# Expert blocks taken by their number inside each expert, with the last stage's first group begun among the final blocks

## The chip, the cores and the metric

One core of a Trainium2 chip runs the whole program in one launch. The metric is the device time in microseconds (us); lower is better. The engines named below are TensorE (PE), VectorE (DVE), ScalarE (ACT), GpSimd (POOL) and SyncE (SP), which only issues DMAs.

## What is computed

`x` has 8192 tokens (128 graphs of 64) of 128 features. Four layers follow each other:

```
x = x + adj @ (LN(x) @ W0) + b0                       # graph layer 0
x = x + FFN0(LN(x))       # attention in each graph; then top 2 of 8 experts (hidden 341) for each token
x = x + norm(adj) @ (LN(x) @ W1) + b1                 # graph layer 1
x = x + FFN1(LN(x))       # top 2 of 6 experts, each three 128x128 layers
```

The part that matters here is the 8-expert layer. For every token, with weights of its two best experts,

```
for e in range(8):
    hh = silu(flat @ w1[e].T) * (flat @ w3[e].T)
    out = out + weights[:, e:e+1] * (hh @ w2[e].T)
```

is needed, and `out` is all that graph layer 1 waits for.

## The kernel before

Tokens are handled in 16 groups of 512 (four tiles of 128). The program has two large parts with a barrier of all five engines between them.

**Part A** (to about 400 us) computes graph layer 0, attention and the choice of experts for all groups. As it goes, POOL scatters each token's row (L358) into `slots_in` in DRAM, at a slot of the chosen expert: each expert has a region of `REG` = 65 rows of blocks, a block being 128 slots, filled in the order of the tokens. At the end the counts are final, and a chain of small DVE instructions (L903 to L924; `link` makes each wait for the one before) turns them into `table`: for each of the `NBLK` = 136 blocks its expert and its row in `slots_in`. The blocks stand expert after expert, the empty ones last. Beside that chain PE runs 18 filler matmuls (L1195) whose results nobody reads; POOL finishes its scatters; SP and ACT write zeros behind each expert's last row. Then comes the barrier (its instructions have the line L243).

**The middle stage** is a pipeline over the 136 blocks. `blocks` calls `block_of(k, u)` on every engine: SP loads block k into `xs` (L1342); PE transposes it (L1930); ACT and DVE split it into a high and a low part (L1488, L1590); PE multiplies by `w13` (L1938); ACT applies silu and DVE the product (L1478, L1595); PE transposes that (L1946) and multiplies by `w2` (L1923); DVE copies the result to `ys` (L1601); SP stores two blocks at a time to `slots_out` (L1345). Blocks 0 to 7 are written out, the rest is a loop of four blocks, and up to `skew` further calls drain the pipeline. During blocks 4 to 7 DVE also does `real_slots`: a token's slot in the region layout becomes its slot in the packed order of `slots_out`. POOL, in `weights()`, loads and splits the weights of the last stage, and then waits.

**The last stage** (`sweep`) runs graph layer 1 and the 6-expert layer, software-pipelined over the 16 groups. Step i of an engine does different work for groups i, i-1, i-2 and so on, in the order of its `body`. For a group g:

- DVE `pick` copies the slots; POOL `gt(0..7)` gathers the two expert rows of each token from `slots_out` (L1427, eight indirect DMAs). For group 0 it first waits until all blocks are stored.
- DVE `add0`, `add1` (L1646, L1655) form x2; `st0`, `mv0`, `var0` its statistics; POOL `rstd0` (L1445) the root; DVE `scale`, `xn_` (L1694).
- PE `aT` (L1968), ACT `tT_` (L1510), PE `gnn` (L1979), with POOL `xb_` (L1437) beside them; DVE `x3` (L1703), `st1`, `mv1`, `var1`; POOL `rstd1` (L1452); DVE `f3_` (L1735). From there on the 6-expert layer, which is nearly all PE's.

PE has filler matmuls `fill(11)`, `fill(10)` and `fill(2)` (L1955) around group 0's `aT`, `gnn` and the transposes of f3 (L1990).

Of the kernel before, what the change touches and what calls it, by code (L numbers as in the profile page):

```python
# [42 lines left out]
C_BLK, C_TRI8 = 592, 592 + NBLK  # L43
# [3 lines left out]
def constants():  # L47
# [14 lines left out]
    c[:, C_BASE:C_BASE + 8] = np.arange(8) * REG * P  # L62
    c[:, C_BLK:C_BLK + NBLK] = np.arange(NBLK)
# [30 lines left out]
def build(nc, x, adj_t, gnn0_w, gnn0_b, ln1, ln2, wqkv, wo, router0, w13, w2, gnn1_w, gnn1_b,  # L94
# [11 lines left out]
    def first(g):  # L106
        return isinstance(g, int) and g == 0

    with ExitStack() as whole:
# [20 lines left out]
        table = sb("table", [1, 2, NBLK], i32)  # L130
        slots_f, gaps = sb("slots_f", [P, NG, 2 * TG]), sb("gaps", [P, 8])


        with ExitStack() as ctx:
# [36 lines left out]
            cnti, nblk = sb("cnti", [P, 8], i32), sb("nblk", [P, 8])  # L171
            tri_nb, cum = sb("tri_nb", [1, 8, 8]), sb("cum", [1, 8])

            past, pastn = (sb(n, [1, NBLK, 8]) for n in ("past", "pastn"))
            bexp, bprev, brow = sb("bexp", [1, NBLK]), sb("bprev", [1, NBLK]), sb("brow", [1, NBLK])
# [67 lines left out]
            with nc.Block() as block:  # L243
# [281 lines left out]
                def _(dve):  # L525
# [370 lines left out]
                    def link(ins):  # L896
# [5 lines left out]
                    dve.wait_ge(router.sem, router.at("car", NG - 1))  # L902
                    link(V.tensor_copy(carry_b[:, :], carry[:, :]))  # L903
# [5 lines left out]
                    link(V.tensor_tensor(tri_nb[:, :, :], nblk[0:1, :].unsqueeze(1).broadcast_to([1, 8, 8]),  # L909
                                         cst[0:1, C_TRI8:C_TRI8 + 64].rearrange("p (a b) -> p a b", a=8), ALU.mult))  # L910
                    link(V.reduce_sum(cum[:, :], tri_nb[:, :, :], AX.X))
                    link(V.tensor_tensor(past[:, :, :], cst[0:1, C_BLK:C_BLK + NBLK].unsqueeze(2).broadcast_to([1, NBLK, 8]),
                                         cum[:, :].unsqueeze(1).broadcast_to([1, NBLK, 8]), ALU.is_ge))
                    link(V.tensor_tensor(pastn[:, :, :], past[:, :, :], nblk[0:1, :].unsqueeze(1).broadcast_to([1, NBLK, 8]), ALU.mult))
                    link(V.reduce_sum(bexp[:, :], past[:, :, :], AX.X))
                    link(V.reduce_sum(bprev[:, :], pastn[:, :, :], AX.X))
                    link(V.tensor_tensor(brow[:, :], cst[0:1, C_BLK:C_BLK + NBLK], bprev[:, :], ALU.subtract))

                    link(V.scalar_tensor_tensor(brow[:, :], bexp[:, :], float(REG), brow[:, :], ALU.mult, ALU.add))
                    link(V.tensor_scalar(table[:, 1, :], brow[:, :], float(P), None, ALU.mult))  # L920
                    link(V.tensor_scalar(table[:, 0, :], bexp[:, :], float(NE0 - 1), None, ALU.min))


                    link(V.tensor_scalar(gaps[:, :], nblk[:, :], -float(REG), float(P), ALU.add, ALU.mult))  # L924
                @block.tensor
                def _(pe):
# [267 lines left out]
                    for n in range(18):  # L1194
                        T.matmul(banks[1][:, 0:2 * P], ident, cst[:, 0:2 * P], start=True, stop=True)  # L1195


        with ExitStack() as ctx:
# [129 lines left out]
            with nc.Block() as block:  # L1328
                @block.sync
                def _(sp):  # L1330
# [16 lines left out]
                    blocks(sp, block_of, 8)  # L1347
# [29 lines left out]
                    def body(g, p):  # L1377
                        lda(g[0], p[0])
                        gst(g[1], p[1])
                        gld(g[1], p[1])  # L1380
                        store(g[2])
                    sweep(sp, body)
# [3 lines left out]
                def _(pool):  # L1386
# [784 lines left out]
```

## Time and profile before

| | us |
|---|---|
| median of 3 runs | 1071.14 |
| their range | 1069.75 to 1075.84 |
| the profiled execution, its own time | 1076.23 |
| its span, first to last instruction | 1074.4 |

PE is busy for 963.5 us (90%) of the span, DVE 721.2, ACT 574.8, POOL 461.3. The span divides into part A (to the barrier at 401), the middle stage (to 697), a passage in which group 0 gets through the start of the last stage (to 730), and the rest of the last stage (to 1074). "Busy" is a share of time in which an engine has an instruction in it; "PEclk" in the rows is the TensorE clock granted, as a share of 2.4 GHz, and is 1.0 or 0.5 at any moment.

### The profile page before, as it was taken

The page shows a single profiled execution, that of the slowest core. Times are in us where ns is not written, and L with a number is a line of the kernel's source. Part 1 is how long each engine was busy: PE and PEld are TensorE (multiplying, and loading weights), DVE is VectorE, ACT ScalarE, POOL GpSimd, SP SyncE. Part 2 cuts the span into 40 slices and gives each one's busy share as a digit, 9 for nine tenths or more (in the row PEclk, how much of TensorE's full clock was granted, in tenths as well). Part 3 has the DMA queues.
Part 4 walks back from the last instruction along what each step waited for, and adds up shares of the span by engine and source line. Part 5 has one row for each costly group of instructions (what it writes and reads, how often), then busy time and mean ns, then how long its engine had stood idle before and what let it go on. Part 6 is the DMA issues. An engine that isn't in the chain of part 4 may idle for free.

```text
span 1074.4 us, 26532 instructions
## 1 busy us (share of the span) xinstructions
PE 963.5 (90%) x6751; PEld 758.7 (71%) x6752; DVE 721.2 (67%) x3045; ACT 574.8 (54%) x1499; POOL 461.3 (43%) x459
## 2 busy tenths in 40 slices
PE   5888888888888759999999999938999999999998
PEld 4776777777776648999999999835555555555564
DVE  4677777677877655555555555427788888888864
ACT  2567667666676514555555555503455555555564
POOL 2256666656666568000000000076565665665510
PEclk9889898889999888999999999968999999999999
DMA  5211111111111014212212212122333433433332
GB/s 195 76 36 42 51 35 42 39 39 48 38 39 32 22 57 110 62 59 66 61 59 66 61 59 66 44 52 62 128 102 105 162 107 98 152 120 101 112 124 79
DMA packets 87453, 80.79 MB, mean 75 GB/s; under 512 B 26766, under 2 KB 80416, under 8 KB 85104
## 3 DMA queue, kind: packets, MB, share of 16 engines
q1 hardware_dynamic: 77472, 61.72, 18.1%
q0 software_dynamic: 8784, 18.16, 5.8%
q10 hardware_dynamic: 1152, 0.39, 0.2%
q8 instruction: 18, 0.29, 0.1%
q14 instruction: 27, 0.22, 0.1%
HBM read 57.50 MB, written 22.74 MB: 75 GB/s over the span
## 4 chain that ended last, share of the span: by engine, by line
PE 39%; issue 11%; POOL 9%; DVE 2%; ACT 1%; DMA 0%; POOLq 0%; DVEq 0%; SPq 0%; ACTq 0%
PE bank L1938 12%; PE bank L1923 9%; POOL expert_rows L1427 7%; PE bank L1946 4%; PE bank L2074 3%; PE bank L2066 3%; PE bank L2042 2%; PE bank L1930 1%; POOL rs_c L1445 1%; PE bank L1979 1%; PE bank L1968 1%; POOL xb_c L1437 1%; PE bank L2009 0%; ACT h L1496 0%; DVE base_all L1703 0%
## 5 line engine op out<-in xcount | busy, mean ns | idle before, releaser
L1427 POOL DMA_INDIRECT expert_rows<-slots_out,slot_c x128 | 140.6, 1099 | 34.9 <-issue 34.9
L1595 DVE TENSOR_TENSOR prod<-bank,act 128x342 f32<-128x342 f32 x136 | 70.0, 515 | 115.6 <-ACT act L1478 115.4
L358 POOL DMA_INDIRECT slots_in<-flat,slot_now x128 | 128.2, 1002 | 43.0 <-issue 43.0
L1426 POOL TENSOR_TENSOR spare_c<-mhalf 128x1 f32<-128x1 f32 x16 | 3.0, 185 | 274.0 <-DMA slots_out<-ys 274.0
L1923 PE MATMUL bank<-w_sb,prodT 128*128 x816 | 119.5, 283 | 0.6 <-DVE ys L1601 0.6
L1478 ACT ACTIVATE act<-bank 128x342 f32<-128x342 f32 x136 | 62.0, 456 | 96.0 <-PE bank L1938 96.0
L1923 PEld LDWEIGHTS bank<-w_sb,prodT 128*128 128x128 f32 x816 | 101.5, 191 | 7.5 <-issue 1.4
L1938 PE MATMUL bank<-w_hi,xT_hi 128*128 x272 | 99.5, 366 | 0.0
L2066 PE MATMUL bank<-h,ew 128*128 128x512 f32 x192 | 97.6, 605 | 0.0
L1938 PE MATMUL bank<-w_hi,xT_lo 128*128 x272 | 87.6, 322 | 0.0
L1938 PE MATMUL bank<-w_lo,xT_hi 128*128 x272 | 87.3, 321 | 0.0
L1503 ACT ACTIVATE h<-bank,eb 128x512 f32<-128x512 f32 x96 | 65.6, 685 | 29.2 <-DVE ys L1752 17.5
L2042 PE MATMUL bank<-f_hi,ew_hi 128*128 128x512 f32 x96 | 66.1, 688 | 6.9 <-ACT h L1496 5.8
L1496 ACT ACTIVATE h<-bank,eb 128x512 f32<-128x512 f32 x96 | 63.6, 680 | 13.8 <-PE bank L2042 13.5
L1946 PE MATMUL bank<-cst,prod 128*128 128x128 f32 x408 | 66.6, 272 | 0.1
L1483 ACT ACTIVATE prodT<-bank 128x384 f32<-128x384 f32 x136 | 66.0, 486 | 0.8 <-PE bank L1946 0.8
L450 ACT ACTIVATE pr<-sc,nmx 128x64 f32<-128x64 f32 x256 | 62.7, 335 | 1.9 <-DVE nmx L683 1.8
L1488 ACT ACTIVATE xT_hi<-bank 128x128 fp32r<-128x128 f32 x136 | 37.7, 278 | 44.5 <-PE bank L1930 44.5
L1590 DVE TENSOR_TENSOR xT_lo<-bank,xT_hi 128x128 fp32r<-128x128 f32 x136 | 39.7, 292 | 25.3 <-ACT xT_hi L1488 16.4
L1452 POOL TENSOR_TENSOR rs_d<-var_d,mhalf 128x4 f32<-128x4 f32 x16 | 18.0, 1124 | 86.4 <-DVE var_d L1727 86.4
L1946 PEld LDWEIGHTS bank<-cst,prod 128*128 128x128 f32 x408 | 52.9, 140 | 2.7 <-DVE prod L1595 0.3
L1938 PEld LDWEIGHTS bank<-w_lo,xT_hi 128*128 128x128 f32 x272 | 52.5, 193 | 0.0
(284 smaller groups left out, 2531.3 us busy)
## 6 DMA issues: line engine op xcount, KB each, us to landing
gate_bc<-gates_dram SPq DMA_DIRECT2D x16, 1536.0 KB
xs<-slots_in SPq DMA_DIRECT2D x136, 64.0 KB, 1.8
slots_out<-ys SPq DMA_DIRECT2D x68, 128.0 KB, 1.9
base_all<-in_x SPq DMA_DIRECT2D x16, 256.0 KB, 2.8
out<-ob SPq DMA_DIRECT2D x16, 256.0 KB
w_lo<-in_w SPq DMA_DIRECT2D x1, 2736.0 KB, 10.1
adjt<-in_adj_t SPq DMA_DIRECT2D x32, 64.0 KB, 2.3
slots_in<-flat,slot_now POOLq DMA_INDIRECT x128
```

The source lines that it names most:

```text
L358: G.indirect_dma_start(out=slots_in, out_offset=bass.IndirectOffsetOnAxis(ap=slot_now[p][:, n:n + 1], axis=0), in_=flat[p][:, n // 2, :], ...
L450: last = S.activation(pr[:, t, h, :], sc[:, t, h, :], ACT.Exp, scale=SCALE, bias=nmx[:, t * NH + h:t * NH + h + 1])
L1427: G.indirect_dma_start(out=rows[p][:, n, :], out_offset=None, in_=slots_out, in_offset=bass.IndirectOffsetOnAxis(ap=slot_now[p][:, n:n + 1 ...
L1483: S.activation(prodT[:, (u - 3) % 2, :], banks[5 + (u - 3) % 2][:, 0:KC * P], ACT.Copy).then_inc(prodT_copied, 1)
L1496: S.activation(h1[n % 3][:, :], banks[B_A[n]][:, :], ACT.Relu, bias=eb1[:, n:n + 1]).then_inc(per["ra"].sem, 1)
L1503: S.activation(h2[n % 3][:, :], banks[B_B[n]][:, :], ACT.Relu, bias=eb2[:, n:n + 1]).then_inc(per["rb"].sem, 1)
L1595: V.tensor_tensor(prod[:, u % 2, 0:HIDP], banks[3 + u % 2][:, 0:HIDP], act1[:, u % 2, :], ALU.mult).then_inc(prod_done, 1)
L1923: last = T.matmul(banks[7][:, 0:C], prodT[:, u % 2, n * P:(n + 1) * P], w2_sb[:, bass.ds(e * (KC * C) + n * C, C)], start=n == 0, stop=n = ...
L1938: last = T.matmul(banks[1 + 2 * n + par][:, 0:HIDP], xx[:, par, :], ww[:, bass.ds(e * (2 * HIDP) + n * HIDP, HIDP)], start=q == 0, stop=q ...
L1946: last = T.transpose(banks[5 + u % 2][:, n * P:(n + 1) * P], prod[:, u % 2, n * P:(n + 1) * P], ident)
L2042: last = T.matmul(banks[B_A[n]][:, :], ww[:, w], ff[p][:, :], start=q == 0, stop=q == 2)
L2066: T.matmul(banks[B_B[n]][:, :], ew2[:, n * C:(n + 1) * C], h1[n % 3][:, :], start=True, stop=True).then_inc(per["b"].sem, 1)
```

## The change

1. The order of the blocks. Before: all blocks of expert 0, then of expert 1, and so on. After: block 0 of every expert that has one, then block 1 of every expert, and so on, empty blocks last. Since the regions are filled in token order, the rows of group g now all lie in the first `filled(g)` = 32(g+1) blocks. The table is found by a longer chain (`dve_t` counts to 27 in place of 17), whose last two links wait for four small new matmuls. PE's fillers at that place become 12, the four matmuls, and 22.
2. `real_slots` has eight steps (blocks 4 to 11) in place of four, since slot numbers are mapped in another way; `pick` of groups 0 and 1 follows at blocks 12 and 13.
3. POOL's gathers for group g wait for `filled(g)` blocks only.
4. `blocks` writes out blocks 0 to 15 and 120 to 135. Between the last ones DVE does `add0` to `xn_` of group 0 and `add0` to `var0` of group 1 (`ahead`), SP loads both groups' `adj`, and after the last h matmuls PE does `aT` and `gnn` of group 0, in banks 0 and 1. `later(g, n)` takes this work out of the sweep.
5. `fill(11)` and `fill(10)` are gone; `fill(8)` stands ahead of the sweep.

```diff
+LEAD, LOOPED = 16, 120
@@ end of part A, DVE
-link(V.tensor_tensor(past[:, :, :], cst[0:1, C_BLK:C_BLK + NBLK].unsqueeze(2).broadcast_to([1, NBLK, 8]),
-                     cum[:, :].unsqueeze(1).broadcast_to([1, NBLK, 8]), ALU.is_ge))
...
+link(V.tensor_tensor(upto[:, :, :], nblk[:, :].unsqueeze(1).broadcast_to([P, MB, 8]),
+                     cst[:, C_JS:C_JS + MB].unsqueeze(2).broadcast_to([P, MB, 8]), ALU.min))
+link(V.reduce_sum(below[:, :], upto[:, :, :], AX.X))
+link(V.tensor_tensor(reached[:, :, :], pos.unsqueeze(2).broadcast_to([P, 2, MB]),
+                     below[:, :].unsqueeze(1).broadcast_to([P, 2, MB]), ALU.is_ge))
+link(V.reduce_sum(row_no[:, :], reached[:, :, :], AX.X))
...
+dve.wait_ge(pe_t, 2)
+link(V.tensor_scalar(table[:, 0, :], banks[2][0:1, 0:2 * P], float(NE0 - 1), None, ALU.add))
+link(V.tensor_scalar(table[:, 1, :], banks[2][0:1, 2 * P:4 * P], float(DUM), float(P), ALU.add, ALU.mult))
@@ middle and last stage
-for k in range(8):
+for k in range(LEAD):
     body(k, k % 4)
-with engine.Fori(2, NBLK // 4) as j:
+with engine.Fori(LEAD // 4, LOOPED // 4) as j:
...
-for k in range(NBLK, NBLK + skew):
+for k in range(LOOPED, NBLK + skew):
     body(k, k % 4)
+def filled(g):
+    return min(8 * TG * (g + 1), NBLK) if isinstance(g, int) else NBLK
+def later(g, n):
+    return None if isinstance(g, int) and g < n else g
@@ POOL, gt
-if first(g):
+if isinstance(g, int) and g < 5:
     for j in range(2):
-        pool.wait_ge(st[j], NBLK // 4 * 16)
+        pool.wait_ge(st[j], filled(g) // 4 * 16)
@@ SP
+if isinstance(k, int) and LOOPED < k <= LOOPED + 2:
+    lda(k - LOOPED - 1, k - LOOPED - 1)
@@ ACT
+if isinstance(k, int) and k == NBLK + 1:
+    tT_(0)
@@ DVE
+def ahead(k):
+    if 4 <= k < 12:
+        real_slots(k - 4)
+    elif k == 12:
+        dve.wait_ge(real, 11)
+        pick(0, 0)
+    elif k == 13:
+        pick(1, 1)
+    elif k == LOOPED:
+        dve.wait_ge(prepared, 8)
+        add0(0, 0)
+    elif k == LOOPED + 1:
+        add1(0, 0)
...
+    elif k == LOOPED + 6:
+        xn_(0)
+    elif k == LOOPED + 11:
+        add0(1, 1)
...
+    elif k == LOOPED + 14:
+        mv0(1)
+        var0(1)
+    elif k == NBLK + 3:
+        x3(0, 0)
+        st1(0)
+        mv1(0)
+        var1(0)
@@ PE
-    if first(g):
-        pe.wait_ge(at["add0"], 1)
-        fill(11)
...
+if isinstance(k, int) and k == NBLK:
+    pe.wait_ge(prepared, 8)
+    pe.wait_ge(lo_done, NBLK)
+    aT(0, 0)
+elif isinstance(k, int) and k == NBLK + 1:
+    pe.wait_ge(prod_done, NBLK - 1)
+    gnn(0)
...
+fill(8)
 sweep(pe, body)
```

PE's fillers at the end of part A. In the kernel before, PE's rows there are:

```order
L1193 MATMUL bank0<-carry_b,oneb 128x8 [waits dve_t]
L1195 MATMUL bank1<-cst 128x256 x18
L243 UNCONDITIONAL_BRANCH
L1909 UNCONDITIONAL_BRANCH [waits barrier_Pool_Activation_PE_DVE_SP_release]
L1930 MATMUL bank0<-cst,xs 128x128 [waits ld_slots0]
```

In the changed kernel:

```order
L1213 MATMUL bank0<-carry_b,oneb 128x8 [waits dve_t]
L1215 MATMUL bank1<-cst 128x256 x12
L1218 MATMUL bank2<-cst,entry 1x128 [waits dve_t]
L1218 MATMUL bank2<-cst,entry 1x128 x3
L1221 MATMUL bank1<-cst 128x256 x22
L247 UNCONDITIONAL_BRANCH
L2008 UNCONDITIONAL_BRANCH [waits barrier_Pool_Activation_PE_DVE_SP_release]
L2029 MATMUL bank0<-cst,xs 128x128 [waits ld_slots0]
```

Sixteen more fillers and the four matmuls on `entry` now stand ahead of PE's arrival at the barrier.

PE from the last blocks into the last stage (`w2_sb` rows are the second expert product, `cst,prod` the transposes, `cst` alone a filler). Before:

```order
L1946 MATMUL bank6<-cst,prod 128x128 x2
L1923 ISA [waits y_copied,prodT_copied]
...
L1923 MATMUL bank7<-w2_sb,prodT 128x128
L1955 MATMUL bank1<-cst 128x256 [waits add0,prepared]
L1955 MATMUL bank1<-cst 128x256 x10
L1968 MATMUL bank2<-adjt_c0,xn_c 128x128 [waits xn,ld_adj_c0]
L1968 MATMUL bank2<-adjt_c0,xn_c 128x128 x3
L1979 MATMUL bank6<-gw1,tT_c 128x128 [waits tT]
L1979 MATMUL bank6<-gw1,tT_c 128x128 x3
L1955 MATMUL bank1<-cst 128x256 x10
L1990 MATMUL bank5<-cst,f3 128x128 [waits f3]
```

After:

```order
L2063 MATMUL bank0<-adjt_c0,xn_c 128x128 [waits ld_adj_c0,xn,lo_done,prepared]
L2063 MATMUL bank0<-adjt_c0,xn_c 128x128 x3
L2022 ISA [waits y_copied,prodT_copied]
...
L2045 MATMUL bank6<-cst,prod 128x128 [waits prodT_copied,prod_done]
L2045 MATMUL bank6<-cst,prod 128x128 x2
L2074 MATMUL bank1<-gw1,tT_c 128x128 [waits tT,prod_done]
L2074 MATMUL bank1<-gw1,tT_c 128x128 x3
L2022 ISA [waits y_copied,prodT_copied]
...
L2053 MATMUL bank3<-cst 128x256 x8
L2083 MATMUL bank5<-cst,f3 128x128 [waits f3]
```

Both graph products of group 0 moved in among the last three `w2` products, and the next thing after the fillers is the transpose of f3.

DVE at the same place (`bank7` to `ys` is a block's result). Before:

```order
L1601 COPY ys<-bank7 128x128 [waits st_slots1,pe_y] x2
L1638 COPY slot_c0<-slots_all 128x8 [waits prepared,real_slots]
L1639 COPY gate_c0<-gates_all 128x8
L1638 COPY slot_c1<-slots_all 128x8
L1639 COPY gate_c1<-gates_all 128x8
L1646 SCALAR_TENSOR_TENSOR x2a<-expert_rows0,gate_c0,base_all 128x128 [waits gathered0]
```

After:

```order
L1644 COPY ys<-bank 128x128 [waits st_slots1,pe_y] x2
L1756 SCALAR_TENSOR_TENSOR base_all<-bank,deg,xb_c 128x128 [waits xb,gnn]
L1756 SCALAR_TENSOR_TENSOR base_all<-bank,deg,xb_c 128x128 x3
L1684 MEMSET spare_d 128x1 [waits x3]
L1764 BN_STATS st_d<-base_all 128x6 x4
```

Behind the last block's copy DVE goes straight to `x3` of group 0.

## Rows read from the trace of the kernel before

**Rows 1.** Stretches: length, busy us (instructions) of each engine, clock, DMA.

```profile
core 0: us, PE busy (x) PEld busy (x) DVE busy (x) ACT busy (x) POOL busy (x), PEclk, DMA share, GB/s
440.00:460.00 20.00, 20.00 (x153) 19.45 (x152) 10.48 (x30) 10.31 (x28) 0.00 (x0) 1.00 0.22 62
700.00:720.00 20.00, 5.35 (x13) 4.31 (x14) 5.29 (x22) 0.00 (x0) 15.31 (x17) 0.50 0.19 50
740.00:750.00 10.00, 9.28 (x36) 6.78 (x35) 7.58 (x48) 5.05 (x9) 4.23 (x6) 0.66 0.19 59
850.00:1000.00 150.00, 148.31 (x589) 87.21 (x588) 129.10 (x598) 82.34 (x145) 92.35 (x88) 1.00 0.38 121
```

**Rows 2.** The barrier's instructions (L243): durations in ns, and when they started.

```profile
L243 PEldq DRAIN  x1: 5490/5490/5490, 394.1 to 394.1; - x1
...
L243 POOLq DRAIN  x1: 1375/1375/1375, 399.6 to 399.6; - x1
...
L243 PEldq EVENT_SEMAPHORE  x1: 51/51/51, 401.1 to 401.1; - x1
```

**Rows 3.** Timeline, end of part A: start, duration, engine, line, shapes, count.

```profile
383.99 0.68 DVE L720 TENSOR_TENSOR base_all<-f,base_all 128x512 f32<-128x512 f32 x1
...
387.96 10.14 PE L1195 MATMUL bank<-cst 128*128 128x256 f32 x36
...
388.81 0.17 DVE L908 CAST nblk<-cnti 128x8 f32<-128x8 int32 x1
...
390.81 1.28 DVE L914 TENSOR_TENSOR pastn<-past,nblk 1x1088 f32<-1x1088 f32 x1
...
392.13 1.27 DVE L915 TENSOR_REDUCE bexp<-past 1x136 f32<-1x1088 f32 x1
```

**Rows 4.** Stretches of one microsecond around the barrier, columns as in rows 1.

```profile
392.00:393.00 1.00, 1.00 (x6) 0.88 (x5) 0.96 (x2) 0.00 (x0) 0.95 (x1) 0.86 0.63 196
...
402.00:403.00 1.00, 0.00 (x0) 0.00 (x0) 0.00 (x0) 0.48 (x1) 1.00 (x5) 0.76 0.03 8
409.00:410.00 1.00, 1.00 (x8) 0.94 (x8) 0.00 (x0) 0.44 (x2) 1.00 (x3) 0.83 0.93 85
```

**Rows 5.** PE's block transposes (L1930): ns min/median/max, first and last start.

```profile
L1930 PE MATMUL bank<-cst,xs x136: 272/273/477, 404.0 to 690.0; 128*128 128x128 f32 x136
```

**Rows 6.** Timeline, DVE between blocks: a step of `real_slots`.

```profile
412.34 1.08 DVE L1609 TENSOR_TENSOR gate_bc<-slots_f,cst 128x896 f32<-128x896 f32 x1
```

**Rows 7.** Timeline, the last block's `w2` product and its copy.

```profile
696.27 0.93 PE L1923 MATMUL bank<-w_sb,prodT 128*128 x6 [0.57 <-DVE ys L1601]
697.24 0.29 DVE L1601 COPY ys<-bank 128x128 f32<-128x128 f32 x1 [1.21 <-PE bank L1923]
```

**Rows 8.** Timeline from the last block to group 0's f3, and on.

```profile
701.38 1.20 POOL L1427 DMA_INDIRECT expert_rows<-slots_out,slot_c  x1 [0.65 <-issue]
...
713.36 1.14 DVE L1646 SCALAR_TENSOR_TENSOR x2a<-expert_rows,gate_c,base_all 128x128 f32<-128x128 f32 x4 [15.53 <-DMA expert_rows<-slots_out,slot_c]
...
718.75 2.89 DVE L1694 TENSOR_SCALAR xn_c<-x,mv_c,xscale 128x128 f32<-128x128 f32 x4
719.75 1.28 POOL L1437 TENSOR_TENSOR xb_c<-x,gb 128x512 f32<-128x512 f32 x1
...
722.09 1.05 PE L1968 MATMUL bank<-adjt_c,xn_c 128*128 128x128 f32 x8
...
723.89 1.16 PE L1979 MATMUL bank<-gw,tT_c 128*128 128x128 f32 x8 [0.75 <-issue]
...
725.09 1.13 DVE L1703 SCALAR_TENSOR_TENSOR base_all<-bank,deg,xb_c 128x128 f32<-128x128 f32 x4 [3.44 <-issue]
...
727.83 1.08 POOL L1452 TENSOR_TENSOR rs_d<-var_d,mhalf 128x4 f32<-128x4 f32 x1 [2.91 <-DVE var_d L1727]
...
732.30 1.01 POOL L1427 DMA_INDIRECT expert_rows<-slots_out,slot_c  x1 [0.30 <-issue]
...
734.65 1.05 POOL L1445 TENSOR_TENSOR rs_c<-var_c,mhalf 128x4 f32<-128x4 f32 x1
```

More of the change, by code:

```diff
@@ L1193, in _ @@
                     T.matmul(banks[0][:, 0:8], oneb[:, :], carry_b[:, :], start=True, stop=True).then_inc(pe_t, 1)
-                    for n in range(18):
+                    for n in range(12):
+                        T.matmul(banks[1][:, 0:2 * P], ident, cst[:, 0:2 * P], start=True, stop=True)
+                    pe.wait_ge(dve_t, 25)
+                    for n in range(4):
+                        last = T.matmul(banks[2][0:1, n * P:(n + 1) * P], entry[:, n // 2, n % 2:n % 2 + 1], ident, start=True, stop=True)
+                    last.then_inc(pe_t, 1)
+                    for n in range(22):
                         T.matmul(banks[1][:, 0:2 * P], ident, cst[:, 0:2 * P], start=True, stop=True)
@@ L1509, in tT_ @@
                                 act.wait_ge(at["gnn"], g)
-                            S.activation(tT[:, :, :], banks[B_AT][:, :], ACT.Copy).then_inc(at["tT"], 1)
+                            S.activation(tT[:, :, :], banks[0 if first(g) else B_AT][:, :], ACT.Copy).then_inc(at["tT"], 1)
                     def hi(g, p):
@@ L1616, in real_slots @@
-                            V.reduce_sum(back, gap, AX.X).then_inc(real, 1)
-                        else:
-                            dve.wait_ge(real, 3)
-                            V.tensor_tensor(slots_all[:, :, :].rearrange("p g s -> p (g s)"), slots, back, ALU.add).then_inc(real, 1)
-                    def block_and_slots(k, u):
-                        block_of(k, u)
-                        if isinstance(k, int) and 4 <= k < 8:
-                            real_slots(k - 4)
-                    blocks(dve, block_and_slots, 4)
@@ L1702, in x3 @@
                             for t in range(TG):
-                                last = V.scalar_tensor_tensor(stream(g, t), banks[B_GNN][:, t * P:(t + 1) * P], deg[p][:, t:t + 1], xb[:, t, :], ALU.mult, ALU.add)
+                                last = V.scalar_tensor_tensor(stream(g, t), banks[1 if first(g) else B_GNN][:, t * P:(t + 1) * P], deg[p][:, t:t + 1], xb[:, t, :], ALU.mult, ALU.add)
                             last.then_inc(at["x3"], 1)
@@ L1750, in m @@
                                 dve.wait_ge(gates_loaded[p], pair(g, p))
+                                if first(g):
+                                    for j in range(2):
+                                        dve.wait_ge(st[j], NBLK // 4 * 16)
                             reused(dve, "c", n, g)
@@ L1884, in body @@
                         dtop_(g[2])
-                        xn_(g[1])
+                        xn_(later(g[1], 1))
                         z_(g[2])
@@ L1967, in aT @@
                             for t in range(TG):
-                                last = T.matmul(banks[B_AT][:, t * P:(t + 1) * P], xn[:, t, :], adjt[p][:, t, :], start=True, stop=True)
+                                last = T.matmul(banks[0 if first(g) else B_AT][:, t * P:(t + 1) * P], xn[:, t, :], adjt[p][:, t, :], start=True, stop=True)
                             last.then_inc(at["aT"], 1)
@@ L1978, in gnn @@
                             for t in range(TG):
-                                last = T.matmul(banks[B_GNN][:, t * P:(t + 1) * P], tT[:, t, :], gw[:, :], start=True, stop=True)
+                                last = T.matmul(banks[1 if first(g) else B_GNN][:, t * P:(t + 1) * P], tT[:, t, :], gw[:, :], start=True, stop=True)
                             last.then_inc(at["gnn"], 1)
-                            if first(g):
-                                fill(10)
                     def f3T(g):
```

155 lines of the change are left out of this document (104 added, 51 removed).

## The prediction, made before the changed kernel was run

> **What bounds the kernel now.** I read the busy shares first, then the chain of work that ended last, then the stretches where that chain leaves PE. In the middle stage PE is busy all 20.00 of 20 us at the full clock, while DVE and ACT are about half idle [rows 1]; the first block's transpose starts at 404.0 and the last at 690.0, 135 steps of 2.12 us [rows 5]. So that stage lasts as long as its matmuls. In most of the last stage it is PE again, 148.31 of 150 us [rows 1]. What is left are two seams. At the barrier all engines stand until 401.1 [rows 2], and the first transpose comes 2.9 us later. Between the middle and the last stage PE works 5.35 of 20 us, at 1.2 GHz, half its clock [rows 1]: the last block is copied at 697.24 [rows 7], the first gather starts at 701.38 once the rows have landed in DRAM, eight gathers follow each other, the first sum waits for them until 713.36 (15.53 us idle on DVE), and then a chain DVE, POOL, DVE, PE, ACT, PE leads to `x3` at 725.09 and to the root ahead of f3 at 727.83 [rows 8]. The chain of waits runs through POOL there. This is the part that the change is about; the barrier is the part that it touches besides.
>
> **The second seam: -26.3 us.** Take `x3` of group 0 as the mark. Before, it starts at 725.09. After, all that leads to it (16 gathers, `add0` to `xn_`, `xb_`, the `adj` loads) stands inside the block stage, and DVE has `x3` directly behind the last copy to `ys`. The two graph products, 1.05 and 1.16 us [rows 8], are now in PE's queue ahead of the last two or three `w2` products, so 2.2 us of work are added to the drain of the pipeline. The drain has gaps of its own, since each `w2` product waits for the copy of the one before (0.57 us idle before the last one, [rows 7]); I take 0.8 us of such gaps as filled, so that the last copy moves from 697.24 to about 698.6 and `x3` starts at about 698.8. 725.1 - 698.8 = 26.3 us. The bounds are the whole 2.2 us on the path with the wait for ACT's copy between the products (0.6 us): 24.9, and none of it: 27.6.
>
> Is something else late next? From `x3` to the root it is 2.74 us in both, all DVE's own work. In the next step POOL does the root, four gathers of group 2 and only then group 1's root, at 734.65, 6.8 us behind 727.83 [rows 8]; DVE's `scale` and `xn_` of group 1 wait for that. The queue of POOL is the same after the change, so that DVE's `add1` to `var0` of group 1, taken out of this step, bring nothing: the step is held by POOL. The later steps have the same instructions in the same order. So the shift is handed on whole.
>
> **The first seam: +6.5 us.** PE ends 18 fillers (36 matmul instructions) 10.14 us after 387.96, that is at 398.1 [rows 3], and its drain ends at 394.1 + 5.5 = 399.6. POOL's drain ends at 399.6 + 1.4 = 401.0, and the release follows at once, at 401.1 [rows 2]. So PE has 1.4 us to spare, no more. The clock rises at about 392.3 (0.86 in that microsecond, [rows 4]); 4.3 us at half and 5.8 at full clock for 36 instructions make (4.3 / 2 + 5.8) / 36 = 0.22 us each at full clock, 0.44 for a filler. After, PE runs 12 fillers, four small matmuls and 22 fillers. The 12 end at about 395.3: ten instructions in the 4.3 us of half clock, 14 at 0.22. Is the DVE chain there by then? Its links 6 to 25 begin, as link 6 did before, at about 389.0, behind the fifth (388.81 + 0.17, [rows 3]): one of 512 elements like L720, 0.68 us; one sum over as many, 1.27 x 512 / 1088 = 0.60; four on 128 elements at about 0.29; and 14 small ones at 0.17 [rows 3]. With 0.04 us between links (390.81 + 1.28 against 392.13) this is 0.68 + 0.60 + 1.16 + 2.38 + 0.80 = 5.6 us, to 394.6. So PE does not wait. The four matmuls have half the columns of a filler, 0.22 us each, 0.9 in all. PE thus does 16 x 0.44 + 0.9 = 7.9 us more, its drain ends at 407.5 and not at 399.6, and the barrier opens 407.5 - 401.0 = 6.5 us later. DVE's last two links, on 256 elements, end near 397.3 and hold nobody. Everything behind the barrier moves with it. The bounds are 5.0, if the clock rises a microsecond or two earlier and the small matmuls cost half; 8.5, if it rises later or PE waits for the chain.
>
> Do the fillers give something back? Before, the clock fell at about 402.5 (0.76, [rows 4]), 4.4 us after the last filler, and came back in the microsecond of 409 (0.83); the first blocks, from about 405.6, ran 3.7 us at half clock, worth 1.9 us. After, PE is idle for about as long: 1.5 us of drain and 2.9 to the first transpose, with a block's real work 1.5 us behind that. I count nothing, and 2 us at best.
>
> **Work put between blocks: +0.8 us, from 0 to 3.** DVE is idle for half of a block's 2.12 us. Before, four steps of `real_slots`, three of them 1.08 us [rows 6], stood there, and PE's pace did not show them. After, there are five of about 1.2 us (1024 elements in place of 896), some short ones, and in blocks 120 to 134 ten pieces of up to 1.14 us (`add0`, [rows 8]). Each puts DVE's next `xT_lo` off by up to a microsecond, which is just about what it has in hand; I take 0.05 us each for 15. POOL's `xb_` is the doubtful one: while it ran for 1.28 us, DVE's `xn_` took 2.89 us, 1.8 more than elsewhere [rows 8]. In the tail it stands at about block 125, once, and could hold one block by 1.3 us.
>
> The Trainium skill ("SBUF — State Buffer", section "Who interferes with whom") explains that stall as an exclusive lock of a port pair that VectorE and GpSimd share, and says that a VectorE instruction with one SBUF input outside its two-port modes is not touched. By that rule the block stage's own DVE work, which reads PSUM and one SBUF operand, passes `xb_` unharmed and the term is nearer 0 than 1.3. The same page (section "SBUF: two separate sides") has a rule against this change: a DMA of the GpSimd queue can wait for its descriptors while VectorE copies in fp32, and it gives 620 ns alone against 3100 ns. Here a gather took 1.01 us beside a busy DVE at 732.30 and 1.20 us with DVE idle at 701.38, so the trace does not show it.
>
> The gathers have room: group 0's begin after block 32, group 1's first four after block 64; the other four follow a root at block 123, with `xb_` between, some 1.05 + 1.28 + 4 x 1.3 = 7.5 us, and landing, against the 17 us to block 131.
>
> **The sum.** -26.3 + 6.5 + 0.8 = -19.0 us. Against the profiled execution's own time that is 1076.2 - 19.0 = 1057.2; this execution lies 5.1 us above the median of the runs, so the median after should be 1071.1 - 19.0 = 1052.1. Its range from the bounds is 1048 to 1057.
>
> **The rivals.**
>
> *The barrier is not held by PE.* If what releases it is not the drain but something that PE's fillers pass unnoticed, the 6.5 us fall away: 1045.6. Against it: the release stands 0.1 us behind the last drain, POOL's [rows 2]. Chance 0.10.
>
> *A colder ramp.* Before, 22 + 20 filler instructions kept PE at work in this passage and it still fell to half clock for about 6.8 of the 10 us from 740 (0.66, [rows 1]), with PE busy 9.28 of them. After, only `fill(8)` stands there, about 3.5 us, and PE waits some 2 us for f3. Where PE is the bound, 6.8 us at half clock cost 3.4 us; two more such stretches would cost 7: 1059. For it: PE's work in the first step is thin. Against: it comes out of the blocks at full clock, not from 17 us of idling. Chance 0.14.
>
> *The waits move into the blocks.* If DVE, in order, stands at `gathered` of group 1 or at group 0's root while the blocks need it, PE stops with it, and most of the gain is lost there: 1066 to 1071. It takes gathers three times as long as in rows 8. Chance 0.05.
>
> *Slower: the pace of the blocks.* Now every block has another expert, and PE's moving operands come from another place of `w13` each time. If that, or DVE's load, cost each of the 136 blocks x us, the change is worth nothing at x = 19.0 / 136 = 0.14 and shows as slower by 0.5% from x = 0.18; at 0.2 us the time is 1079. Against: the weights are in SBUF, the address is taken from a register at every block before the change too, and a pace of 2.12 us over 286 us, eight experts among them, leaves no place for a cost of changing. Chance 0.04.
>
> **The numbers.** The forecast has 0.67, the colder ramp 0.14, the free barrier 0.10, the moved waits 0.05, the slower blocks 0.04. A difference under 0.5% (5.4 us) can't be told from none. Faster: 0.67 + 0.14 + 0.10 = 0.91; same: 0.05; slower: 0.04. The range runs from the free barrier with a better second seam, 1044, to the colder ramp with the upper bounds, 1061.
>
> **What the profile after would show.** Right: PE's drain at the barrier ends near 407.5 and the release with it; the pace of the transposes stays at 2.12 us; DVE shows no idle time before `add0` in blocks 120 and 131; `x3` of group 0 within 1.7 us of the last copy's start; from there to the second group's root 9.6 us as before; the rest of the last stage as long as before. Wrong: a barrier at 401, transposes at more than 2.2 us apart anywhere outside the first blocks, a half clock for more than 10 us behind the last block, or a longer time from the first f3 to the end.

## The result, and the profile after

The changed kernel took 1062.15 us (median of 5 runs, 1058.44 to 1064.47), the kernel before beside it 1074.02 us (1069.75 to 1075.84): ratio 0.9897, 95% interval 0.9864 to 0.9929, so 11.9 us less where 19.0 were forecast. It is faster by more than 0.5%, but lies 1.15 us above the range. (The forecast of 1052.1 started from three runs with a median of 1071.1; from the 1074.0 of the pair it would be 1055.0, so 2.9 of the 10 us between forecast and time are the start's, and 7.1 the change's.) The profiled execution took 1058.44 us, with a span of 1056.6.

Some of the difference between the two profiled executions has nothing to do with the change: part A, in which POOL has the same program in both, ended 6.9 us earlier after (POOL's drain starts at 392.7 against 399.6, [rows 2]). So I compare stage by stage. The barrier in the kernel after, as in rows 2: duration in ns, then when it started.

```profile
L247 PEldq DRAIN  x1: 4048/4048/4048, 395.7 to 395.7; - x1
...
L247 PEldq EVENT_SEMAPHORE  x1: 51/51/51, 399.9 to 399.9; - x1
```

PE's drain ends at 399.7 and the release follows at 399.9; POOL's drain was over at 392.7 + 1.4 = 394.1. PE now holds the barrier, by 5.7 us. From its first matmul beside the chain (381.5 after, 388.0 before) to the end of its drain PE took 18.3 us where it was 11.6, so 6.7 more. The block transposes, which answer to rows 5:

```profile
L2029 PE MATMUL bank<-cst,xs x136: 272/273/476, 403.0 to 700.9; 128*128 128x128 f32 x136
```

First to last is 297.8 us, where it was 286.0: 11.8 us more, where the forecast had 0.8. The seam behind them, from the timeline of after (start, duration, engine, line), which answers to rows 7 and 8:

```profile
709.48 0.29 DVE L1644 COPY ys<-bank 128x128 f32<-128x128 f32 x1 [1.31 <-PE bank L2022]
709.69 1.12 DVE L1756 SCALAR_TENSOR_TENSOR base_all<-bank,deg,xb_c 128x128 f32<-128x128 f32 x4
...
712.42 1.05 POOL L1490 TENSOR_TENSOR rs_d<-var_d,mhalf 128x4 f32<-128x4 f32 x1 [29.15 <-DVE var_d L1780]
```

`x3` starts 0.2 us behind the last copy's start and 8.8 us behind the last transpose; before, 35.1 us lay between transpose and `x3`. That is the forecast -26.3, to the tenth. From group 0's root to the end it is 344.2 us against 346.6.

So the sum is 5.7 + 0.2 (release to first transpose) + 11.8 - 26.3 - 2.4 = -11.0, against -11.9 between the medians. One term is wrong: the block stage. The pitch, from one block's transpose to the next, lies between 2.04 and 2.56 us behind the first block, but for three places: blocks 38 to 40 with 3.79, 7.26 and 3.58 us, blocks 70 and 71 with 4.38 and 2.38, block 127 with 3.47. Transposes more than 2.2 us apart were one of the prediction's signs of being wrong, though single pitches of up to 2.35 us stand in the kernel before too. The first place in stretches of 2 us (columns as in rows 1):

```profile
482.00:484.00 2.00, 2.00 (x18) 1.99 (x17) 0.92 (x4) 0.95 (x3) 1.69 (x2) 1.00 0.24 57
484.00:486.00 2.00, 1.68 (x13) 1.42 (x11) 0.33 (x1) 0.16 (x1) 1.39 (x3) 1.00 0.39 107
486.00:488.00 2.00, 0.91 (x7) 0.84 (x7) 0.58 (x2) 0.28 (x1) 1.67 (x2) 1.00 0.26 66
488.00:490.00 2.00, 1.40 (x8) 0.97 (x7) 0.00 (x0) 0.00 (x0) 1.42 (x2) 1.00 0.23 66
490.00:492.00 2.00, 0.07 (x1) 0.07 (x2) 0.51 (x1) 0.46 (x1) 1.62 (x2) 0.91 0.26 66
492.00:494.00 2.00, 1.10 (x4) 0.71 (x5) 0.51 (x2) 0.99 (x4) 0.00 (x0) 0.50 0.12 33
```

DVE and ACT stop first, then PE, and only POOL (fifth pair of numbers) goes on. The clock falls to half at 491.6, behind the gaps in PE's work, so it isn't what started them; it stays there for 6.8 us. What POOL does there, from its timeline:

```profile
481.50 1.20 POOL L1465 DMA_INDIRECT expert_rows<-slots_out,slot_c  x1 [0.65 <-issue]
483.00 1.02 POOL L1465 DMA_INDIRECT expert_rows<-slots_out,slot_c  x1 [0.31 <-issue]
484.33 1.01 POOL L1465 DMA_INDIRECT expert_rows<-slots_out,slot_c  x1 [0.30 <-issue]
...
490.92 1.01 POOL L1465 DMA_INDIRECT expert_rows<-slots_out,slot_c  x1 [0.31 <-issue]
```

These are group 0's eight gathers, each as short as in the last stage. The other two places are group 1's first four gathers (557 to 562 us) and its last four (677 to 683: one, then `xb_`, then three in a row). What the engines wait for from 480 to 500 us (us in total, times, longest):

```profile
DVE prod L1638 <- issue: 3.5, 1, 3.5
DVE ys L1644 <- remote: 3.4, 2, 2.2
ACT act L1516 <- issue: 3.4, 1, 3.4
ACT xT_hi L1526 <- remote: 3.1, 1, 3.1
```

"remote" and "issue" mean that nothing in this core's record ended the wait: the transpose whose semaphore ACT's `xT_hi` waits for started at 484.12 and took 0.27 us, and `xT_hi` starts at 487.25. Work is done, and word of it comes late.

### The profile page after: what moved, and what is told of

Its sections match the earlier page's. It is cut to its first block, busy times and chain, and to the rows that moved or that the text cites. A ratio compares the mean times of both kernels' runs of the same rounds, so it can differ in the third digit from the quotient of the medians.

```text
span 1056.6 us, 26375 instructions
## 1 busy us (share of the span) xinstructions
PE 953.9 (90%) x6765; PEld 751.2 (71%) x6766; DVE 720.0 (68%) x3063; ACT 575.2 (54%) x1499; POOL 461.7 (44%) x459
## 4 chain that ended last, share of the span: by engine, by line
PE 38%; issue 11%; POOL 7%; DVE 3%; ACT 1%; DMA 1%; another core or an unknown queue 1%; POOLq 0%; DVEq 0%; SPq 0%; ACTq 0%
PE bank L2037 12%; PE bank L2022 9%; POOL expert_rows L1465 5%; PE bank L2045 4%; PE bank L2167 3%; PE bank L2159 2%; PE bank L2135 2%; PE bank L2029 1%; PE bank L2074 1%; POOL rs_c L1483 1%; PE bank L2063 1%; DMA gate_bc<-gates_dram 1%; DVE base_all L1756 1%; ACT h L1533 1%
## 5 line engine op out<-in xcount | busy, mean ns | idle before, releaser
L1483 POOL TENSOR_TENSOR rs_c<-var_c,mhalf 128x4 f32<-128x4 f32 x16 | 20.8, 1297 | 127.2 <-DVE var_c L1732 125.6
```

## The experiments

The kernels of one session ran on one chip, with the kernel before beside them. The sessions fell into two kinds, which turned out to be the heart of the matter: in some the kernel before takes 1072 to 1074 us, as in the recorded result, in the others 1050 to 1052. I call them sessions of 1074 (three, with that of the result) and of 1050 (five). Runs of one session stand together in the table: e_order to e_direct; c_after and e_best; c_after2 and e_many; c_after3 to e_spaced2; e_direct2 to e_pairs; then c_after4 with e_direct3, and c_after5 with e_direct4. Each median is of 4 runs (e_order: 10). The stage is the time from the first to the last block transpose in the profiled execution.

| run | session | median us | ratio, 95% interval | stage us |
|---|---|---|---|---|
| e_order | 1050 | 1049.95 | 0.998 (0.996 to 1.000) | 288.5 |
| e_fill6 | 1050 | 1022.60 | 0.970 (0.967 to 0.974) | 288.1 |
| e_spaced | 1050 | 1027.28 | 0.976 (0.973 to 0.979) | 285.4 |
| e_direct | 1050 | 1030.17 | 0.978 (0.975 to 0.981) | 285.0 |
| c_after | 1050 | 1027.00 | 0.978 (0.974 to 0.982) | 285.3 |
| e_best | 1050 | 1025.59 | 0.974 (0.969 to 0.978) | 288.3 |
| c_after2 | 1050 | 1027.95 | 0.977 (0.973 to 0.982) | 284.4 |
| e_many | 1050 | 1027.97 | 0.978 (0.975 to 0.982) | 285.5 |
| c_after3 | 1074 | 1063.59 | 0.990 (0.986 to 0.993) | 296.4 |
| e_fill6b | 1074 | 1057.85 | 0.985 (0.982 to 0.988) | 297.7 |
| e_spaced2 | 1074 | 1055.28 | 0.980 (0.975 to 0.985) | 287.6 |
| e_direct2 | 1074 | 1047.03 | 0.979 (0.975 to 0.982) | 285.4 |
| e_best2 | 1074 | 1043.68 | 0.973 (0.972 to 0.975) | 285.8 |
| e_pairs | 1074 | 1043.04 | 0.974 (0.971 to 0.976) | 286.7 |
| c_after4, c_after5 | 1050 | 1031.61, 1026.45 | 0.979, 0.975 | 284.2, 285.0 |
| e_direct3, e_direct4 | 1050 | 1027.71, 1029.23 | 0.978, 0.979 | 285.1, 287.4 |

**The order of the blocks alone (e_order).** The early work goes back behind the last block:

```diff
-                return min(8 * TG * (g + 1), NBLK) if isinstance(g, int) else NBLK
+                return NBLK
-                return None if isinstance(g, int) and g < n else g
+                return g
-LEAD, LOOPED = 16, 120
+LEAD, LOOPED = 16, 136
```

with the 12 + 6 fillers, with `fill(11)` and `fill(10)` again in place of `fill(8)`, and without the adjacency loads, DVE's pieces and the two graph products among the blocks.

> The new order of the blocks alone: the table, slots and real_slots code of the change and its 12 + 6 fillers, but no gather, sum, adjacency load or graph product inside the block stage; all of them follow the last block as before. Theory A (something that runs beside the blocks costs the 11.8 us; the order itself is free): 136 blocks again at 2.12 us, first to last transpose 287 us (286 to 289), last transpose to x3 near 35, so 1071 + (0 to 2) = 1072 us (1068 to 1076). Rival B (the order of the blocks, or the repeated and empty blocks in it, makes some of them slow): the long pitches at blocks 38 to 41 and 70 stay, first to last transpose 295 to 298 us, 1080 us.

The time is that of the kernel before (0.998), and the stage 288.5 us, without a pitch over 2.5. The order costs nothing that this can tell, and the slower rival of the prediction is gone. That the expected microseconds were some 20 too high throughout was the first sign of the two kinds of session.

**6 fillers (e_fill6).**

```diff
-                    for n in range(22):
+                    for n in range(6):
```

> The changed kernel with 6 fillers instead of 22 after the four table matmuls. Both theories of the block stage say the same of it: PE no longer holds the barrier between the parts, which is released by POOL, 5 to 6 us earlier, and the block stage stays as it is with its 11.8 us. 1062 - 5.7 = 1056.5 us (1055 to 1058). Rival: with fewer fillers the clock is still low when the blocks begin and rises later, which takes back up to 4 us of it: 1060.

It had the same bursts of gathers (several in a row, 0.3 us apart) as the changed kernel, and no stall. So the stall is not a property of the instructions alone.

**Gathers one by one (e_spaced).** In POOL's program, ahead of the sweep, and taken out of it for these two groups:

```diff
+                    for g in range(2):
+                        for n in range(8):
+                            for j in range(2):
+                                pool.wait_ge(st[j], (filled(g) + 4 * n) // 4 * 16)
+                            gt(n, g, g)
```

> The changed kernel, but the eight gathers of group 0 and the eight of group 1 are issued one at a time, one for each four finished blocks (from block 32 and block 64 on), instead of in bursts. Theory A1 (a burst of back to back gathers delays the engines' semaphores): no pitch over 2.6 us at blocks 38 to 41, 70 and 127; first to last transpose 288 us instead of 298; 1062 - 10 = 1052 us (1050 to 1054). Rival A2 (each gather costs the blocks a fixed time, 12 us over 16 gathers, 0.7 us each): the long pitches become sixteen smaller ones, the stage stays at 296 to 298 us and the time at 1062.

**Plain copies (e_direct).**

```diff
+                            if isinstance(g, int) and g < 2:
+                                pool.dma_start(rows[p][:, n, :], slots_out[n * P:(n + 1) * P, :]).then_inc(gathered[p], 16)
+                                return
                             G.indirect_dma_start(out=rows[p][:, n, :], ...
```

> The changed kernel with the sixteen gathers of groups 0 and 1 replaced by plain copies of the same 128 x 128 tiles by the same queue of POOL, at the same places (the rows that these two groups add up are the wrong ones). If the stall comes from the indirect form (descriptors made from a list of row numbers, 128 rows taken one by one): it goes, 1062 - 10 = 1052 us. If it comes from what POOL's queue carries at all, or from reading a tensor while it is being written: it stays, 1062 us (1060 to 1064).

Neither shows a stall, but with e_fill6 beside them this tells nothing apart. The changed kernel itself had to be run again.

**The changed kernel again (c_after), and both edits (e_best).**

> The changed kernel itself again, beside the kernel before on whichever chip this falls. Theory A (the 11.8 us in the block stage belong to the change: its gathers beside the blocks): long pitches at blocks 38 to 41, 70 and 127 again, stage 296 to 298 us, ratio to before 0.989 (0.986 to 0.993). Rival C (the stall is not the change's but of that chip or that load of the program, since the same gathers in the kernel with 6 fillers ran with no pitch over 2.6 us): no long pitch, stage 286 to 288 us, ratio 1052.15 - (-5.7 - 1.5 + 26.3 + 2.4 = 21.5) over 1052.15 = 0.980 (0.977 to 0.983).

> Both edits on the changed kernel: 6 fillers instead of 22 after the table matmuls, and the sixteen gathers of groups 0 and 1 one for each four finished blocks. If the fillers hold the barrier by 5.7 us in every run, this is 5 to 6 us faster than the spaced kernel (0.976), ratio 0.971 (0.968 to 0.974), and equal to the kernel with 6 fillers alone where no stall occurs; if spacing also avoids a stall where one occurs, 10 us more against the changed kernel beside it.

Rival C: no long pitch, stage 285.3, ratio 0.978. e_best was 1.4 us faster than the changed kernel here, not 5 to 6; the two intervals overlap, so this pair doesn't size the fillers. Its profile has the gain at the barrier (the release 0.2 us behind the end of POOL's drain, 5.9 in c_after) and loses 3.0 us of it in the stage (288.3). The other two profiles with 6 fillers in sessions of 1050 have the same stage, 288.1 and 288.5, and a pitch of 2.13 to 2.14 us over blocks 10 to 135 against 2.11; of the nine with 22 fillers only e_direct4 is like them. With 6 fillers in sessions of 1074, without a stall, it was 285.8 and 286.7. No run says what sets this.

**Again, and 32 more gathers (c_after2, e_many).**

```diff
+                    for m in range(4):
+                        for n in range(8):
+                            G.indirect_dma_start(out=rows[1][:, n, :], ...  # rows of group 0, block 32 on
+                        pool.wait_ge(extra, 128 * (m + 1))
                     sweep(pool, body)
```

> The changed kernel once more, to see whether the stall in the block stage follows the kernel or the chip or load it runs on. If it is of the chip or load: no pitch over 2.7 us among the blocks and ratio 0.978 where the kernel before takes about 1050 us; long pitches at the gathers again and ratio 0.989 only where the kernel before takes about 1074. If it comes at random: either, whatever the kernel before takes.

> The changed kernel with 32 more gathers on POOL's queue, back to back in four rounds of eight, into the second buffer, from block 32 on and before the real gathers of group 0. If a burst of gathers by itself delays the engines (theory A1), 32 of them give long pitches from block 34 on: at 8 gathers for 8.4 us, 20 to 34 us more, ratio about 1.00. If a burst does nothing to the blocks on an undisturbed chip (rival C), the blocks keep 2.12 us and the ratio is that of the changed kernel, 0.978 (0.975 to 0.981).

In a session of 1050, 32 gathers more in four bursts cost nothing: stage 285.5, 0.978 against 0.977. There a burst is free.

What is different in a session of 1074? The code of part A is the same everywhere but for its end, and its waits tell. Before, in the recorded session, from 60 to 360 us:

```profile
DVE var_b L622 <- remote: 21.9, 13, 1.8
ACT v_diag L438 <- remote: 20.7, 13, 1.7
DVE nmr L632 <- POOL rs_b L323: 20.4, 13, 1.6
```

The same stretch of c_after has no "remote" at all; its list goes on where these lines would stand:

```profile
POOL spare L361 <- DVE slots_f L849: 29.7, 15, 3.4
DVE nmr L636 <- POOL rs_b L327: 26.0, 13, 2.1
PEld bank L1086 <- ACT pr L454: 19.3, 14, 1.4
```

13 waits of 1.7 us each, 21.9 in all, are as long as what lies between the two kinds of session (22 to 24 us), and it does lie in part A: POOL's drain at its end is over between 394.1 and 401.6 us in the eight profiles of the kind of 1074 and between 374.3 and 378.9 in the twelve of the kind of 1050, 21.8 us apart in the mean, while from `x3` to the end both have 345 to 349 us. Their place is seen in the timeline of the kernel after, recorded session, POOL and DVE:

```profile
199.94 1.05 POOL L362 DMA_INDIRECT slots_in<-flat,slot_now  x1 [0.18 <-issue]
201.29 0.97 POOL L362 DMA_INDIRECT slots_in<-flat,slot_now  x1 [0.30 <-issue]
202.57 0.97 POOL L362 DMA_INDIRECT slots_in<-flat,slot_now  x1 [0.30 <-issue]
203.85 0.97 POOL L362 DMA_INDIRECT slots_in<-flat,slot_now  x1 [0.30 <-issue]
205.13 0.97 POOL L362 DMA_INDIRECT slots_in<-flat,slot_now  x1 [0.30 <-issue]
```

```profile
205.11 0.28 DVE L616 BATCH_NORM_AGGREGATE mv_b<-st_b 128x2 f32<-128x6 f32 x3
205.31 0.19 DVE L765 TENSOR_TENSOR oh<-topf,cst 128x64 f32<-128x64 f32 x1
207.08 0.17 DVE L626 TENSOR_SCALAR var_b<-mv_b 128x4 f32<-128x4 f32 x1 [1.58 <-remote]
```

Five scatters follow each other, and behind them DVE waits 1.58 us for a semaphore that its own instruction, over at 205.4, had to raise. In c_after, with five scatters at the same place, the same instruction follows at once:

```profile
199.29 0.20 DVE L765 TENSOR_TENSOR oh<-topf,cst 128x64 f32<-128x64 f32 x1
199.41 0.17 DVE L626 TENSOR_SCALAR var_b<-mv_b 128x4 f32<-128x4 f32 x1
```

The longest such wait stands at the end of part A, where the changed kernel's chain waits for its four new matmuls and 13 scatters follow each other. In the kernel after, recorded session, and in c_after:

```profile
388.99 1.03 PE L1218 MATMUL bank<-cst,entry 128*1 128x128 f32 x8
392.99 0.41 DVE L942 TENSOR_SCALAR table<-bank 1x256 int32<-1x256 f32 x1 [4.80 <-remote]
```

```profile
369.29 1.03 PE L1218 MATMUL bank<-cst,entry 128*1 128x128 f32 x8
370.44 0.41 DVE L942 TENSOR_SCALAR table<-bank 1x256 int32<-1x256 f32 x1 [1.93 <-PE bank L1218]
```

All seven profiles of a changed kernel in sessions of 1074 have it, with 4.7 to 5.1 us, and none of the others. It cost the recorded kernel nothing, since DVE's drain was over at 394.1, with POOL's, and PE's at 399.7; but with 6 fillers DVE and POOL end together, and a little more would be paid.

**Three kernels side by side in a session of 1074 (c_after3, e_fill6b, e_spaced2).**

> The changed kernel again, on whichever chip this falls. Theory D (semaphores freeze beside indirect transfers under the conditions of the recorded runs only, already in the kernel before: 13 waits of DVE and ACT put down to remote, 21.9 us, in its first part): where the kernel before takes about 1050 us, none of these waits and ratio 0.978; where it takes about 1074, these waits in the first part, long pitches among the blocks, ratio 0.989.

> The changed kernel with 6 fillers instead of 22, beside the changed kernel on the same chip. The barrier term says 5 to 5.7 us less (ratio to before 0.973 where the changed kernel has 0.978). Under the recorded conditions theory D says that it stalls among the blocks as the changed kernel does.

> The changed kernel with the gathers of groups 0 and 1 one for each four blocks, beside the changed kernel on the same chip. Where the kernel before takes about 1050 us: equal within 2 us. Under the recorded conditions: 8 to 10 us faster than the changed kernel if a burst is what freezes, equal to it if each gather freezes by itself.

The changed kernel repeats the recorded result: ratio 0.990, pitches of 3.89, 7.19 and 2.84 us at blocks 38 to 40, 4.43 at 70, 3.51 at 127. With 6 fillers it stalls in the same places (stage 297.7) and is 5.7 us faster. With the gathers one by one it does not stall. Its transposes in e_spaced2, and those of c_after3 ahead of them:

```profile
L2029 PE MATMUL bank<-cst,xs x136: 272/273/447, 411.3 to 707.7; 128*128 128x128 f32 x136
```

```profile
L2034 PE MATMUL bank<-cst,xs x136: 272/273/447, 409.0 to 696.7; 128*128 128x128 f32 x136
```

The stage is 287.6 against 296.4 us and the time 8.3 us less, although part A of e_spaced2 has its "remote" waits as before:

```profile
DVE var_b L626 <- remote: 21.9, 13, 1.8
ACT v_diag L442 <- remote: 20.6, 13, 1.7
```

So what stalls the blocks is gathers in a row, in such a session; the same sixteen with gaps show no stall. How many in a row it takes is not settled: in part A and in the last stage runs of three show no late semaphore, but at block 127 the stall of 1.4 us came behind one gather, `xb_` and three.

**Form and number (e_direct2, e_best2, e_pairs).** The last is e_best with

```diff
-                                pool.wait_ge(st[j], (filled(g) + 4 * n) // 4 * 16)
+                                pool.wait_ge(st[j], (filled(g) + 8 * (n // 2)) // 4 * 16)
```

> The sixteen gathers of groups 0 and 1 as plain copies of the same tiles on POOL's queue, in the same bursts (the rows that these two groups add up are the wrong ones), on a second chip. Where the kernel before takes about 1050 us: no long pitch, ratio 0.978 as on the first. Where it takes about 1074: if the indirect form is what freezes the semaphores, no pitch over 2.7 us at blocks 38 to 41, ratio 0.981 or below; if any burst of POOL's descriptors does, pitches of 3.9, 7.2 and 2.8 us again and ratio 0.990.

> 6 fillers and the gathers of groups 0 and 1 one for each four blocks. Where the kernel before takes about 1074 us: 1063.6 - 8.3 - 5.7 = 1049.6, ratio 0.975 (0.972 to 0.979), no long pitch. Where it takes about 1050: ratio 0.974 as on the first such chip.

> As the kernel with both edits, but the gathers in pairs, two back to back for each eight blocks. Under the recorded conditions: if a freeze needs three or more in a row (the first part's runs of three scatters show none, its runs of five do), no long pitch and the time of the kernel beside it within 1.5 us; if each second gather freezes, eight pitches 1 to 2 us longer and 8 to 12 us more. Elsewhere: the time of the kernel beside it.

This was a session of 1074 (before: 1072.13 us) again. e_direct2 has the "remote" waits in part A, where the scatters are as they were,

```profile
DVE var_b L626 <- remote: 20.3, 13, 1.7
```

and none in the block stage, where eight plain copies stand in a row: stage 285.4. Its ratio is 0.979, where the changed kernel had 0.990 in both sessions of this kind. Pairs of gathers do not stall either (286.7) and take the time of single ones. e_best2 is 28.5 us faster than the kernel before; 24.4 was expected, from another session. The changed kernel was not run beside these three, so that its blocks would have stalled there is inferred from the waits of part A alone, for all three kernels.

**A pair for the form (c_after4 and 5, e_direct3 and 4).** For that reason the changed kernel and the plain copies were run together, twice.

> The changed kernel beside the kernel with plain copies, on one chip. Where the kernel before takes about 1074 us: long pitches and ratio 0.990. Where it takes about 1050: neither, ratio 0.978.

> The plain copies in place of the sixteen early gathers (the rows that two groups add up are the wrong ones), beside the changed kernel on the same chip. If the indirect form is needed for the stall: where the kernel before takes about 1074 us, no long pitch and 10 to 12 us less than the changed kernel; where it takes about 1050, equal to it within 2 us.

> The changed kernel beside the kernel with plain copies, once more, since the last pair fell on a chip where the kernel before takes 1051 us. Where it takes about 1074: long pitches and ratio 0.990. Where it takes about 1050: neither, ratio 0.978.

> The plain copies in place of the sixteen early gathers (the rows that two groups add up are the wrong ones), beside the changed kernel. Indirect form needed: where the kernel before takes about 1074 us, no long pitch and 10 to 12 us less than the changed kernel. Any burst: the same stall and time as the changed kernel.

Both were sessions of 1050, and nothing stalled: 1031.61 and 1027.71, then 1026.45 and 1029.23, differences of both signs. That the indirect form is needed therefore rests, as far as times go, on e_direct2 against the changed kernel of other sessions.

The traces hold a second mark of such a session that bears on it. Each transfer raises its semaphore 16 times. Of the 2048 raises of part A's 128 scatters, the profiles of the kind of 1050 have 2043 to 2048 on record, those of the kind of 1074 only 918 to 947. Of the 256 raises of the sixteen early transfers, sessions of 1074 have 103 to 109 where the gathers stand in bursts (after, c_after3, e_fill6b), 158 with pairs, and all 256 with single gathers and with plain copies (e_spaced2 and e_best2; e_direct2); sessions of 1050 have 241 to 256. So in e_direct2 itself the scatters of part A are of the disturbed kind and the plain copies, though in bursts, are not. It is the same order as that of the stalls, but a record with gaps is not a time, and the form stays likely and not shown. Nor do these runs tell whether the recording of semaphores itself has a part in the waits.

The last session bore the same chip number as that of e_direct2 and e_best2, and the kernel before took 1051.57 us in it, not 1072.13. If the number means the same chip, the kind of session is not the chip's; what it is, the runs don't say.

## Why the prediction was wrong

- **What bounds the kernel** held: PE in the block stage and in the last stage (147.90 of 150 us from 850 on, [rows 1]), and two seams.
- **The second seam, -26.3**: right. 26.3 in the recorded pair, and 8.7 to 8.8 us from the last transpose to `x3` in every run that has the early work.
- **The first seam, +6.5**: the mechanism right, the size 5.7, within its bounds. PE had 6.7 us more to do where the sum had 7.9, and the other engines' drains left it 1.0 us and not 1.4 (394.1 lies 12.6 us behind PE's first matmul, 13.0 before). With 6 fillers the release goes back to the other engines' drains, and in one session e_fill6b was 5.7 us faster than c_after3.
- **The last stage as long as before**: 2.4 us shorter in the recorded pair, with the steps behind group 1's start unchanged; from `x3` to the end it varied between 345.1 and 348.9 us from run to run of one and the same kernel, so the 2.4 us can be chance.
- **Work put between blocks, +0.8, from 0 to 3**: this is the step that failed. It measured +11.8 in the recorded session (10.4 in c_after3) and about -1 in sessions of 1050 (stage 284.2 to 285.3 against 286.0, which is the kernel before in a session of 1074; e_order, with `real_slots` alone between its blocks, had 288.5). DVE's pieces and `xb_` cost next to nothing: from block 118 to the end c_after has pitches of 2.05 to 2.34 us, the kernel before 2.05 to 2.22. The failure is in what I priced there: the DVE pieces one by one, and the sixteen gathers only by whether they would land in time. Their price for the others I took from their own duration, 1.01 us beside a busy DVE [rows 8], and that was just as short while the blocks stood still.
- The nearest rows for it were not in the last stage but in part A, where the scatters are indirect transfers of POOL in rows of five: 13 waits without a cause in the record, 21.9 us in all. I read part A only for where it ends. With 1.7 us for each of three bursts the bound would have been about 5 us, still less than the 11.8, of which the eight gathers alone made 8.3; but "a wait with no releaser" would have been a rival with a price.
- **The rivals.** The barrier is held by PE, the ramp was not colder (half clock for 3.4 us behind the blocks), the waits did not move by the path that I named (a late `gathered`), and the order of the blocks costs nothing that can be told. The stall that came was none of them.
- **What was luck.** The kind of session wasn't foreseen, and the forecast of -19.0 lies between what the two kinds gave: -11.9 and -10.4 in sessions of 1074, -22.9, -23.0, -19.5 and -25.1 in sessions of 1050. With the stall-free stage (-1) and the seams as measured (-26.3, +5.7) the sum is -21.6, and -24.0 with the last stage's 2.4.

The Trainium skill ("SBUF — State Buffer", section "SBUF: two separate sides") was weighed as a rule against the change: a GpSimd DMA can wait for its descriptors while VectorE copies in fp32 from SBUF to SBUF. The row that the prediction held against it doesn't test it, since beside the gather at 732.30 DVE ran statistics (L1663) and no copy, and DVE's copies of block results read a bank. No gather got longer in the stall (1.01 us), so the rule isn't what stopped the blocks: VectorE and ScalarE wait while GpSimd's transfers are issued at full speed.

A better version has 6 fillers and the early gathers singly: 0.973 of the kernel before in a session of 1074 (e_best2; 0.974 in pairs) and 0.974 in one of 1050 (e_best). The changed kernel has 0.990 in sessions of 1074; in those of 1050 it has 0.975 to 0.979, which can't be told from 0.974.

## What to carry to other kernels

Before moving transfers beside other work, look in the trace at what stands beside the same kind of transfer now, and take every wait that has no releaser as a price to be explained. Issue indirect transfers with gaps when a pipeline of short semaphore hand-offs runs beside them: it cost nothing where it wasn't needed (e_spaced 0.976, c_after 0.978, in two sessions) and was worth 8 us here. Where a time doesn't repeat on another day, run the unchanged kernel again before explaining the changed one.

## What the runs showed of the hardware

- In sessions where the kernel before took 1072 to 1074 us, semaphores reached waiting engines 1.5 to 5 us late during a run of indirect transfers from POOL, an engine's own among them: behind five scatters in a row (13 times, 1.7 us each), beside thirteen (4.7 to 5.1 us), within eight gathers (8.3 us of pitch over three blocks, part of it at half clock), within four (2.5 us), and behind one, a POOL instruction and three (1.4 us). Runs of one and two never did, nor did runs of three scatters, nor the bursts of up to four gathers in the last stage, where no wait is put down to "remote"; there PE has long matmuls queued, but whether that is the reason was not tested. In sessions of 1050 not even 32 more gathers did.
- The transfers are not issued more slowly during a stall, 1.01 us each, and the engines' costliest instructions have the same median durations in c_after and c_after3, within 2%.
- A stall leaves a half clock behind: in the recorded run the granted clock fell to 1.2 GHz behind 2 us in which PE was busy for 0.07, and stayed there for 6.8 us; in c_after3 and e_fill6b for 3.4 us.
